# Combining, the next norm, the scores and most of h by tile in one stage; beta and the attention vectors made in other stages

## The reference

```
x = x + L0_gnn(layernorm(x))      # three diffusion steps over a graph of 1024 nodes
x = x + L0_ffn(layernorm(x))      # 64 experts, top 2, then layernorm * gamma + beta
x = x + L1_gnn(layernorm(x))      # two graph attention layers, 8 heads each
x = x + L1_ffn(layernorm(x))      # 8 experts, top 1

# L0_ffn, cut:
out = sum_k w_k * (relu(x @ W1[e_k] + b1[e_k]) @ W2[e_k] + b2[e_k]) + x
return (out - mu) * rsqrt(var + EPS) * gamma + beta
# one graph attention layer, cut (concat, self loops in the edges):
h = (x @ W).reshape(N, heads, out_ch)
a_src = einsum('nhc,hc->nh', h, att_src);  a_dst = einsum('nhc,hc->nh', h, att_dst)
e = leaky_relu(a_src[src] + a_dst[dst], 0.2)
alpha = softmax of e over the edges of each dst
out = segment_sum(h[src] * alpha, dst) + bias
```

## Time and profile before

| | us |
|---|---|
| median of three runs | 1385.2 (1382.22 to 1386.55) |
| profiled execution: time | 1385.21 |
| profiled execution: span | 1383.3 |
| granted TensorE clock, mean | 0.868 of full speed |

### The profile page before, as it was taken

How to read it: one execution, slowest core, us unless ns; L and a number is a source line. 1 busy time by engine, 2 the same in 40 slices (tenths; PEclk the granted TensorE clock), 3 DMA queues, 4 the chain that set the end, 5 groups by cost and what they waited for, 6 DMA issues and landing times. The chain is left out here.

```text
span 1383.3 us, 17351 instructions
## 1 busy us (share of the span) xinstructions
PE 1081.4 (78%) x5488; PEld 748.7 (54%) x5488; DVE 772.0 (56%) x1626; ACT 515.1 (37%) x710; POOL 624.4 (45%) x501
## 2 busy tenths in 40 slices
PE   4999379761899999979388987977998787715695
PEld 2444267551677777749345877874644342215472
DVE  6888475646233333318647777752596775484233
ACT  2332434220111111102235767774376667831010
POOL 1000645104555555535025867782377677601543
PEclk9999699955899999985589999999999999955796
DMA  3000000073588999816020111111111111008454
GB/s 103 0 1 0 1 0 0 1 237 143 161 295 298 305 305 303 266 65 208 0 93 10 53 31 47 32 32 61 33 32 45 31 46 30 23 0 276 151 204 138
DMA packets 110553, 140.59 MB, mean 102 GB/s; under 512 B 31076, under 2 KB 73668, under 8 KB 110488
## 3 DMA queue, kind: packets, MB, share of 16 engines
q1 hardware_dynamic: 94008, 114.54, 25.4%
q0 software_dynamic: 16480, 25.24, 5.4%
HBM read 138.71 MB, written 29.81 MB: 122 GB/s over the span
## 5 line engine op out<-in xcount | busy, mean ns | idle before, releaser
L1476 POOL TENSOR_TENSOR am<-CT,qb 128x1024 f32<-128x1024 f32 x128 | 299.4, 2363 | 61.1 <-ACT PT L1496 40.0
L1589 DVE TENSOR_TENSOR am<-PS,am 128x1024 f32<-128x1024 f32 x128 | 156.5, 1223 | 73.1 <-ACT PS L1489 68.4
L1489 ACT ACTIVATE PS<-adb,ab 128x1024 f32<-128x1024 f32 x128 | 143.0, 1117 | 90.0 <-DVE am L1589 90.0
L1057 DVE COPY yo<-PS 128x512 f32<-128x512 f32 x79 | 54.6, 691 | 207.1 <-PE PS L995 207.1
L1583 DVE CUSTOM_DVE_ANT_0 masked<-PS,mask 128x1024 f32<-128x1024 f32 x128 | 156.1, 1220 | 20.7 <-issue 17.6
L1703 PE MATMUL PS<-h,PT 128*128 128x129 f32 x1024 | 134.2, 291 | 30.8 <-ACT PT L1496 24.7
L987 PE MATMUL PS<-xgT,w1r 128*128 128x128 f32 x1264 | 155.9, 277 | 0.0
L987 PEld LDWEIGHTS PS<-xgT,w1r 128*128 128x128 f32 x1264 | 149.3, 194 | 1.7 <-issue 1.7
L1703 PEld LDWEIGHTS PS<-h,PT 128*128 128x128 f32 x1024 | 128.9, 204 | 38.6 <-issue 37.2
L1022 ACT ACTIVATE hT<-PS,b1T 128x128 f32<-128x128 f32 x158 | 49.3, 363 | 268.7 <-PE PS L987 268.7
L995 PE MATMUL PS<-w2r,hT 128*128 128x512 f32 x316 | 148.4, 593 | 0.0
(11 more groups left out here) (310 smaller groups left out, 1615.2 us busy)
## 6 DMA issues: line engine op xcount, KB each, us to landing
w1r<-in_L_ffn_W SPq DMA_DIRECT2D x79, 512.0 KB, 4.8
w2r<-in_L_ffn_W SPq DMA_DIRECT2D x79, 512.0 KB, 6.2
adb<-a_scratch SPq DMA_DIRECT2D x16, 512.0 KB, 3.9
qb<-q_scratch SPq DMA_DIRECT2D x14, 512.0 KB, 3.7
wc<-in_L_gnn_W SPq DMA_DIRECT2D x16, 256.0 KB, 4.0
x_res<-in_x SPq DMA_DIRECT2D x1, 2048.0 KB, 9.5
W1t<-in_L_gnn_W SPq DMA_DIRECT2D x2, 1024.0 KB, 6.9
W2t<-in_L_gnn_W SPq DMA_DIRECT2D x2, 1024.0 KB, 7.1
```

The lines of the kernel that those rows point to most:

```text
L1476: pool.tensor_tensor(am[:, k % RING, :], CT[:, s, :], qb[:, hd % 2, :], ALU.add).then_inc(s_sum, 1)
L1489: act.activation(RELU, adb[:, hd % 2, :], ACT.Relu, bias=ab[:, s, hd:hd + 1]).then_inc(s_relu, 1)
L1589: dve.tensor_tensor(am[:, k % RING, :], RELU, am[:, k % RING, :], ALU.add).then_inc(s_all, 1)
```

## The change

The work on the attention vectors moves into a class Vectors. Its loads are issued by SP in the last diffusion step; chunks 0 to 4 are made at the start of ln1, 5 and 6 in rt0 before the choice of experts is waited for, 7 to 15 after the ranks. All 16 chunks now lie at once where the first experts' weights go, so first_experts loads the second weights first and each first weight after two more chunks are turned. Beta is added to x by POOL during the experts, one tile after each of eight transfers. The combine block now does, for each tile, the sum, its norm with gamma and residual, the norm of the next block (ln2 is gone), the transposes, the scores ab and, for tiles 0 to 6, 768 of h's 1024 columns. Its bias products stand three tiles ahead of their use. a1 keeps six h units: two before the pairs, four between them. In attend, for a1 and a2 alike, q_row(0) and a_row(1) change places, A_ROW moves one pair and Q_AFTER two pairs later; in a1 alone normed moves behind the second pair.

```diff
-        def layernorm(name, src, xln, xT, loaded=None):
+        def layernorm(name, src, xln, xT, loaded=None, vectors=None):
                 @block.scalar
                 def _(act):
+                    if vectors is not None:
+                        vectors.move_att(act)
+                        vectors.move(act, 0, 5)
                     act.wait_ge(s_stat, 1)
                     act.activation(sq[:], ve[:], ACT.Sqrt).then_inc(s_sqrt, 1)
...
                 @block.tensor
                 def _(pe):
+                    if vectors is not None:
+                        vectors.turn_att(pe)
+                        vectors.products(pe, 0, 5)
...
+        class Vectors:
...
+            def products(self, pe, first, last):
+                self.turned(pe, first)
+                pe.wait_ge(self.s_attm, 1)
+                for i in range(first, last):
+                    if i + 1 < last:
+                        self.turned(pe, i + 1)
+                    self.summed(pe, i)
...
+            def move(self, act, first, last):
+                for i in range(first, last):
+                    act.wait_ge(self.s_wt, i + 1)
+                    if i >= 2:
+                        act.wait_ge(self.s_v, i - 1)
+                    act.copy(self.wct[:, i % 2, :], PS[:, 5 + i % 2, :]).then_inc(self.s_wtm, 1)
...
         with nc.Block() as block:
+            @block.sync
+            def _(sp):
+
+                sp.wait_ge(s_sum, 2 * NT)
+                vectors.load(sp)
...
+            V_FIRST, V_AHEAD = 5, 7
...
+                    sp.dma_start(xs[N * K:N * K + P, :], xln[:, 0, :]).then_inc(s_behind, 16)
                     prefetch(sp)
-                    sp.dma_start(xs[N * K:N * K + P, :], xln[:, 0, :]).then_inc(s_behind, 16)
                     sp.wait_ge(s_behind, 16)
...
+                    if vectors is not None:
+                        vectors.products(pe, V_FIRST, V_AHEAD)
                     pe.wait_ge(s_pick, 1)
...
+                    if vectors is not None:
+                        vectors.products(pe, V_AHEAD, len(vectors.chunks))
                     pe.wait_ge(s_sw, 1)
...
         def first_experts(sp):
...
+            for e in range(WR - 1):
+                second(e)
             for e in range(WR):
-                load_weights(sp, ins["L0_ffn_W1"], ins["L0_ffn_W2"], slice(e, e + 1), e, s_w0)
+                sp.wait_ge(vectors.s_wt, 2 * e + 2)
+                sp.dma_start(w1r[:, e, :, :], ins["L0_ffn_W1"][e:e + 1].rearrange("o (k p) h -> p (o k) h", p=P)
+                             ).then_inc(s_w0[e], 16)
+            sp.wait_ge(vectors.s_v, len(vectors.chunks))
+            second(WR - 1)
...
+                        if beta_d is not None and 2 * LAG <= e < 2 * LAG + NT:
+                            t = e - 2 * LAG
+                            pool.wait_ge(s_beta, 16)
+                            pool.tensor_tensor(x[:, t, :], x[:, t, :], beta[:], ALU.add)
...
+                def bias(t):
+                    if t >= 3:
+                        pe.wait_ge(s_o, t - 2)
+                    pe.matmul(PS[:, t % 3, :], r0["swT"][:, t * P:(t + 1) * P], r0["b2s"][:], start=True,
+                              stop=True).then_inc(s_bias, 1)
+
+                for t in range(3):
+                    bias(t)
                 for t in range(NT):
...
+                    pe.wait_ge(s_xln, t + 1)
+                    if t:
+                        pe.wait_ge(s_xtm, t)
+                    for k in range(KD):
+                        mm = pe.transpose(PS[:, 3, k * P:(k + 1) * P], xln[:, t, k * P:(k + 1) * P], ident[:])
+                    mm.then_inc(s_xt, 1)
+                    if t + 3 < NT:
+                        bias(t + 3)
+                    pe.wait_ge(s_xtm, t + 1)
+                    own = slice(t * P, (t + 1) * P)
+                    for k in range(KD):
+                        mm = pe.matmul(PS[:, 7, t * 2 * HEADS:(t + 1) * 2 * HEADS], xT[:, k, own], v1[:, k, :],
+                                       start=(k == 0), stop=(k == KD - 1))
+                    mm.then_inc(s_ab, 1)
+                    if t == NT - 1:
+                        continue
...
+                    for k in range(KD):
+                        mm = pe.matmul(PS[:, 4 + t % 2, :], xT[:, k, own], W1t[0][:, k, :],
+                                       start=(k == 0), stop=(k == KD - 1))
+                    mm.then_inc(s_h, 1)
...
+                    for k in range(KD):
+                        mm = pe.matmul(PS[:, 6, q], xT[:, k, own], W1t[1][:, k, :],
+                                       start=(k == 0), stop=(k == KD - 1))
+                    mm.then_inc(s_hq, 1)
...
+                root(0)
                 for t in range(NT):
...
+                    act.wait_ge(s_stat2, t + 1)
+                    act.activation(sq2[:, t:t + 1], ve2[:, t:t + 1], ACT.Sqrt).then_inc(s_sqrt2, 1)
+                    if t + 1 < NT:
+                        root(t + 1)
+                    act.wait_ge(s_rs2, t + 1)
+                    act.activation(xln[:, t, :], x[:, t, :], ACT.Identity, bias=nmr2[:, t:t + 1],
+                                   scale=rs2[:, t:t + 1]).then_inc(s_xln, 1)
+                    if t:
+                        h_moved(t - 1)
+                    act.wait_ge(s_xt, t + 1)
+                    act.copy(by_tile(xT, t), PS[:, 3, :].rearrange("p (k n) -> p k n", k=KD)).then_inc(s_xtm, 1)
...
+                def added(t):
+                    o = o0[:, t % 4, :]
+                    if t == 0:
+                        dve.wait_ge(s_gb, 16)
+                    link(dve.scalar_tensor_tensor(o, o, mv[:, t, 0:1], gamma[:], ALU.subtract, ALU.mult))
+                    dve.wait_ge(s_sqrt, t + 1)
+                    rooted(one(ve, t), one(sq, t), one(tq, t))
+                    link(dve.tensor_scalar(one(tq, t), one(tq, t), 0.5, None, ALU.mult))
+                    link(dve.reciprocal(one(rs, t), one(tq, t)))
+                    link(dve.scalar_tensor_tensor(x[:, t, :], o, one(rs, t), x[:, t, :], ALU.mult, ALU.add))
+                    link(dve.bn_stats(st2[:, t, :], x[:, t, :]))
+                    link(dve.bn_aggr(mv2[:, t, :], st2[:, t, :]))
...
+                summed(0)
                 for t in range(NT):
...
+                    added(t)
+                    if t + 1 < NT:
+                        summed(t + 1)
+                    scaled(t)
+                dve.wait_ge(s_ab, NT)
+                dve.tensor_copy(ab[:].rearrange("p t h -> p (t h)"), PS[:, 7, 0:NT * 2 * HEADS])
...
+                H0 = 2
+                H_AT = (0, 1), (0, 5), (1, 1), (2, 1)
...
-                     {1: (1,), 2: (2,), 3: (3,), 4: (4, 5), 5: (6,), 6: (7,)})
+                     {0: (1,), 2: (2,), 3: (3,), 4: (4, 5), 5: (6,), 6: (7,)})
...
-            A_ROW = {1: 2, **{8 * (hd - 3) + 5: hd for hd in range(3, HEADS)}}
-            Q_AFTER = {4: 1, 7: 2, **{NT * (hd - 1): hd for hd in range(3, HEADS)}}
+            A_ROW = {1: 2, **{8 * (hd - 3) + 6: hd for hd in range(3, HEADS)}}
+            Q_AFTER = {4: 1, 7: 2, **{NT * (hd - 1) + 2: hd for hd in range(3, HEADS)}}
...
-                        if hd and s == (4 if final else 0):
+                        if hd and s == (4 if final else 1):
                             normed(hd - 1)
...
-                        if i == H0 - 3:
+                        if i == (H0 - 3 if final else H0 - 1):
+                            q_row(0)
                             a_row(1)
-                            q_row(0)
...
-        layernorm("ln2", x, xln, xT)
...
+        attend("a1", KD, CH1, xT, W1t, None, v1, h1, ins["L1_gnn_b1"], a_dram[0], q_dram[0], False)
```

More of the change, by code:

```diff
@@ L667, in _ @@
                                        accum_out=sm[:, t:t + 1]).then_inc(s_exp, 1)
+                    if vectors is not None:
+                        vectors.move(act, V_FIRST, len(vectors.chunks))
                     act.wait_ge(s_tw, 1)
-                    act.copy(swT[:], PS[0:X0, 6:8, :].rearrange("p a n -> p (a n)")).then_inc(s_twm, 1)
+                    act.copy(swT[:], PS[0:X0, 0:2, :].rearrange("p a n -> p (a n)")).then_inc(s_twm, 1)
                 @block.vector
@@ L890, in loop, with experts @@
                 body(NX0 - WR + j, NX0 // WR - 1, j, j == WR - 1)
-        v1 = place("v1", [P, KD, 2 * HEADS], F32, 96 * KIB)
-        v2 = place("v2", [P, KF, 2 * HEADS], F32, 96 * KIB + 256)
-        def experts(tag, blocks, table, W1_d, W2_d, b1_d, xs, ys, rows, loop, s_w, fetched, owner=None, picked=None):
+        beta = place("beta", [P, D], F32, 32 * KIB)
+        def experts(tag, blocks, table, W1_d, W2_d, b1_d, xs, ys, rows, loop, s_w, fetched, owner=None, picked=None,
+                    beta_d=None):
             NX = b1_d.shape[0]
@@ L1170, in build @@
-        s_yb, s_gb = [sem(f"c0_yb{j}") for j in range(4)], sem("c0_gb")
-        s_bias, s_sum, s_stat, s_sqrt, s_chain = (sem("c0_" + k) for k in ("bias", "sum", "stat", "sqrt", "chain"))
```

(37 more changed lines are left out.)

354 lines of the change are left out of this document (204 added, 150 removed).

## The result

The changed kernel takes 1345.8 us (median of four runs, 1343.0 to 1350.6) against 1384.2 us: ratio 0.973, 95% interval 0.969 to 0.976. Run again it gave 1346.1 us and 0.970 (0.966 to 0.973).

A forecast was written before the change was run, and what follows sets the result against it. The kernel was taken as a row of stages on one core, with no engine bound throughout. 1385.2 + 6 - 5 - 6 - 25 + 0.5 - 7 = 1349 us; range 1332 to 1371, 0.85 of the chance.

The forecast's parts named there:

- ln1: Stage with five vector chunks ahead of its work: ACT's square root starts later, cost +6.0 us (bounds +3 and +8).
- The cover after the ranks: Nine chunks fall into PE's waits of 11.61 and 20.45 us: cost 0, up to +2 if thinner.
- Combine block: Combine, norm and scores by tile: DVE 8.15 us, PE 7.5 at full clock; -5 us (bounds -11 and +5).
- SP's 2 MB of W1: 0 to +1: Combine stage: W1's loads replace 1.5 MB of other loads while yb arrives, 0 to +1 us.
- 0.65 us a tile: Combine stage: PE's cold first tile costs 3 to 4 us, of which PE gains back 0.65 a tile.
- Rivals 1 and 3: Combine stage: 1, PE stays at 1.2 GHz, 1394 us, chance 0.06; 3, cold part of its time, 1364 us, 0.12.
- Head of a1: Stage start to first exp: score products go, 34 us against 40, -6 us (bounds -3 and -9.5).
- Pairs of a1: a1's heads: six h units go, normed moves, 22.2 us a head, q late; -25 us (bounds -14 and -31).
- Rivals 2 and 4: a1's heads: 2, held by q's round trip or DVE, 1360 us, chance 0.20; 4, no gain, 1375 us, 0.05.
- a2's steps: a2's heads: a_row behind the sixth gather, four heads gain 1.5 to 2 us each, -7 (bounds +2 and -12).
- a2's start: a_row and q_row swap: DVE's maxima begin 2 us later under ACT's wait for h, +0.5 us.

## Why the prediction was right, and where it was not

- **ln1: right, +5.9 for +6.0.** Chunk, table load and queueing on ACT were as priced. The cover after the ranks is thinner than I read: I had the swT copy done 5 us before the scatter is through; in one trace of after it was done 5 us before the scatter's last issue and 11 us before x0's block, in the other 4 us behind that issue and 1.3 us before the block. Two kernels that moved chunks there lost the 6 us again.
- **Combine block: sum right, three terms off.** DVE's pace was 7.74 for 8.15 us a tile, seven tiles giving 2.9 us. "SP's 2 MB of W1: 0 to +1" was 3.7: a load issued before the gathers holds their rows. PE did not regain what its cold start cost, as I had it do by 0.65 us a tile, because both engines took 7.74 us: from the last first sum to a1 it took 19 us, and a quarter row shortened by 1.3 us a tile took 4.6 off that. Rivals 1 and 3 fell with the windows at 1.00 from 652 on.
- **Head of a1: -4.7 for -6.** The two products at half clock were right (3.79 and 3.78 us); the first maximum came 6.0 us after the start, where I had 5. I listed the q row ahead of head 1's row without asking what the other order gives; the swap cost 5.1 us.
- **Pairs of a1: -28.1 for -25.** The mechanism was right: units out of the pairs, normed behind the second sum, q late from about the fifth head (22.9 and 23.0 in the fifth and sixth steps, in the second trace 21.7 and 23.0). A head was 21.6, not 22.2, and putting normed back cost 2.3 us a head, 1.95 of them the wait. But I read the h unit's cost in the wait before normed only; the second wait, for the row product behind the unit, shows only when the first is removed. Rivals 2 and 4 fell.
- **a2's steps: -8.1 for -7.** Right, and by elimination it is the row product's move.
- **a2's start: +7.1 for +0.5. This step failed.** I wrote that DVE's maxima would begin 2 us later "under ACT's wait for h". There is no such cover: head 1's maxima come 4.0 to 4.4 us later, behind POOL's q, the q row and the row itself. Cut in three, the stretch reads as follows. From a1's last normed pass to a2's first maximum it takes 27.5 us for 25.4: the order there is the same, and the 32 score products take 16.8 and 16.3 us in the traces of after, 15.2 to 15.6 in before, with the swap back and with the shorter quarter row. From there to head 1's first maximum it takes 20.3 for 15.9; with the swap in the kernel but a higher clock it is 19.4 (0.91 for 0.87, in the kernel with the shorter quarter row), so the order costs 3.5 and the clock up to 0.9. The rest takes 49.5 for 49.0. That makes 3.5 us of order and some 3 of clock. The whole stretch alone would not tell them apart: it took 92.6 us with the swap put back and 92.2 with the swap in and the shorter quarter row.

In the profiled runs this step cost 6.6 us more than I had, and a1's pairs (3.1), a2's steps (1.1) and the combine block (1.1) gave more than I had: the sum came out near because errors cancelled. That it lay within 3 us is luck to that extent; no mechanism of the forecast ties them.

## What to carry to other kernels

When two products feed different consumers, put first the one whose consumer has the most work queued before the common goal, not the one that the goal names. Price a heavy block on an in-order engine by everything that stands behind it, not by the one wait that shows: the next wait appears when that one goes. And cut both traces at the same events before believing a small difference of medians.

## What the runs showed of the hardware that I had not expected

- Gathered rows issued 0.3 us behind the first of three bulk loads were in use 9.0 us after their issue; without the loads in front DVE used them 3.8 us sooner.
- The granted clock of the same instructions differs from trace to trace: a2's start, in kernels with the same order there, has 0.89 in both traces of the changed kernel and with tile 6's products moved (96.3 to 97.4 us), 0.91 with two chunks in ln1, with q earlier and with normed put back (95.0 to 95.2), 0.93 with W1 behind the rows (94.0) and 0.94 with the shorter quarter row (92.2). That is up to 5 us without an edit nearby; with one trace of each, it stays open whether it belongs to the kernel or to the execution.
- A result of PE can reach its waiting engines 5 to 10 us after the modelled end of its instruction: 341.1 and 346.1, 340.6 and 350.2 above. The changed kernel has it in one trace and not in the other, and every edited kernel with the changed rt0 has it.
